# An LSTM step in which the input and cell gates take both halves of the state at once

## The reference

```python
# L0                                   # L1, per step
h = tanh(h @ Wh + x_t @ Wx + b)        h_bar = x_t @ Wx + b + h @ Wh
                                       i, f, o = sigmoid of h_bar[:, 0:256], [256:512], [512:768]
                                       g = tanh(h_bar[:, 768:1024])
                                       c = f * c + i * g;  h = o * tanh(c)
# L2: gates from means over the stream, two of four experts, and
shared = gelu(x @ sw1 + sb1) @ sw2 + sb2
# L3: adapters whose low-rank matrices come from cond
```

## Time and profile before

| | before |
|---|---|
| median of the runs (3, lowest to highest) | 1118.36 us (1118.17 to 1118.6) |
| profiled execution, its own time | 1117.36 us |
| its span, first to last instruction | 1115.4 us |
| mean granted clock of TensorE | 0.974 of full speed |
| busy: PE | 1079.2 us, 97% |
| busy: PEld | 979.4 us, 88% |
| busy: DVE | 818.1 us, 73% |
| busy: ACT | 586.4 us, 53% |
| busy: POOL | 279.3 us, 25% |

### The profile page before, as it was taken

The page is one execution under the profiler, slowest core; times in us unless marked ns, Lnnn a source line. Parts: engine busy times, 40 slices in busy tenths (PEclk is TensorE's granted clock), DMA queues, the critical chain, the costliest instruction groups (busy, mean ns, idle before and its releaser), DMA issues. The chain is left out here.

```text
span 1115.4 us, 54596 instructions
## 1 busy us (share of the span) xinstructions
PE 1079.2 (97%) x21946; PEld 979.4 (88%) x21946; DVE 818.1 (73%) x3458; ACT 586.4 (53%) x2147; POOL 279.3 (25%) x861
## 2 busy tenths in 40 slices
PE   6889999999999999999999998899999999999998
PEld 5889999999999999999999987688888888888877
DVE  7667877877877877777777676686666666676697
ACT  4456666566566566566565543433333333334486
POOL 3523323323333333333333320380000000000041
PEclk8759999999999999999999999999999999999999
DMA  8302120120220100000001110000000000000022
GB/s 258 103 23 59 56 63 25 56 65 23 61 60 26 57 18 29 14 23 23 9 4 27 16 15 12 1 2 2 2 2 2 2 1 2 2 3 2 4 90 82
DMA packets 54913, 36.91 MB, mean 33 GB/s; under 512 B 25560, under 2 KB 53514, under 8 KB 54668
## 3 DMA queue, kind: packets, MB, share of 16 engines
q1 hardware_dynamic: 54060, 33.12, 10.4%
q10 hardware_dynamic: 608, 0.30, 0.1%
HBM read 28.42 MB, written 4.98 MB: 30 GB/s over the span
## 5 line engine op out<-in xcount | busy, mean ns | idle before, releaser
L611 ACT ACTIVATE gel<-bank,seq 128x256 f32<-128x256 f32 x256 | 121.5, 475 | 214.7 <-PE bank L1253 211.9
L1251 PE MATMUL bank<-XHL,WE 128*128 128x256 f16 x768 | 209.9, 273 | 8.2 <-DVE XHL L842 3.4
L1251 PE MATMUL bank<-GH,WE 128*128 128x256 f16 x768 | 209.1, 272 | 2.4 <-DVE GH L868 2.0
L1253 PE MATMUL bank<-XHL,WE 128*128 128x256 f16 x768 | 209.8, 273 | 0.0
L1252 PE MATMUL bank<-XHL,WE 128*128 128x256 f16 x768 | 209.7, 273 | 0.0
L1253 PE MATMUL bank<-GH,WE 128*128 128x256 f16 x768 | 209.4, 273 | 0.0
L1252 PE MATMUL bank<-GH,WE 128*128 128x256 f16 x768 | 209.3, 273 | 0.0
L1363 PE MATMUL bank<-LH,seq 128*128 128x16 f16 x6144 | 194.4, 170 | 9.9 <-DVE LH L908 9.6
L1363 PEld LDWEIGHTS bank<-LH,seq 128*128 128x128 f16 x6144 | 171.5, 96 | 30.1 <-DVE LH L908 14.1
L428 POOL TENSOR_TENSOR RH<-rf,RH 128x32 f16<-128x32 f32 x256 | 63.7, 249 | 420.0 <-ACT RH L568 419.8
L1253 PE MATMUL bank<-seq 128*128 128x64 f16 (+2 forms) x1088 | 163.7, 208 | 0.0
(11 more groups left out here) (210 smaller groups left out, 2641.2 us busy)
## 6 DMA issues: line engine op xcount, KB each, us to landing
stage<-in_L_cond_ew SPq DMA_DIRECT2D x64, 128.0 KB, 2.1
stage<-in_L_cond_W SPq DMA_DIRECT2D x32, 256.0 KB, 3.6
XHL<-in_x SPq DMA_DIRECT2D x8, 512.0 KB, 9.0
out<-WE SPq DMA_DIRECT2D x16, 256.0 KB, 2.2
stage<-in_L_cond_sw SPq DMA_DIRECT2D x2, 1024.0 KB, 6.2
scratch<-rows SPq DMA_DIRECT2D x96, 8.0 KB, 2.1
stage<-in_L_cond_Wx SPq DMA_DIRECT2D x1, 1024.0 KB, 9.0
stage<-in_L_cond_Wh SPq DMA_DIRECT2D x1, 1024.0 KB, 11.1
```

The source lines that it names most:

```text
L611: nc.scalar.activation(gel[:, m % 2, :], banks[m % len(banks)][:, 0:256], ACT.Gelu_apprx_tanh, scale=scale, bias=bias).then_inc(s["a_g"], 1)
L1251: MM(out_, w(HI), x(HI), start=start, stop=False, skip_group_check=True)
L1253: return MM(out_, w(HI), x(LO), start=False, stop=stop, skip_group_check=True)
```

## The change

**The gates.** Each of the four tiles of input and cell gate takes 2 matmuls of 16 columns with the low half of the weights (line 1401 of the changed kernel) and 2 of 32 columns in which the state's high and low half stand side by side under the high half of the weights (1412). They leave two partial sums in PSUM. TensorE's order in a step is: input and cell gate with the low weights, the forget gate's high by high products (1407), the wait for `hl`, the 8 paired ones, `pe_ig`; the rest of the forget gate (1417, 1418), `pe_f`; the output gate as before (1425, 1429). That makes 36 matmuls a step in place of 44. VectorE's new `lstm_sum` (line 920, `zig`) adds the two sums, ScalarE takes one tangent of the forget gate (`tf`) and one of `zig` (`tig`).

**PSUM and x products.** Input and cell gate now fill two banks, the forget gate has one bank of four slots, the output gate one of two slots, each slot one turn of 4 steps. So the output gate's x products are made for 4 steps at a time, the seeds are three kinds, and TensorE has new waits: for the forget seed ahead of line 1407 (step 3 of each turn), for the output seed ahead of 1425 (step 1), for `oz` ahead of the output gate's x products, for a forget tangent ahead of the forget gate's.

**Order.** `lstm_sum` is the first instruction of a step on VectorE, `shared_lo` stands right behind it (it was behind the state update of the step before), and `HALVES` moves filling between steps.

```diff
-FIG_TILES = [2, 3, 0, 1, 6, 7]
+IG_TILES = [0, 1, 6, 7]
+F_TILES = [2, 3]
 O_TILES = [4, 5]
+NIG = len(IG_TILES)
+TURNS = T // H
+F_SLOTS, O_SLOTS = 4, 2
...
-        FIG, OB = bank[0:2], bank[2:4]
+        IG, FB, OB = bank[0:2], bank[2], bank[3]
         RB, HB, YB = bank[4], bank[5:7], bank[7]
...
                 n = blk * U + u
-                act.wait_ge(s["pe_fig"], n + 1)
-                nc.scalar.activation(tfig[:], FIG[u // H % 2][:, 0:6 * H * B].rearrange(
-                    "p (m t b) -> p m t b", m=6, t=H)[:, :, u % H, :],
-                    ACT.Tanh, scale=0.5 / S_LSTM).then_inc(s["a_fig"], 1)
+                act.wait_ge(s["pe_f"], n + 1)
+                slot = n // H % F_SLOTS
+                z = FB[:, slot * C * H * B:(slot + 1) * C * H * B].rearrange("p (m t b) -> p m t b", m=C, t=H)
+                nc.scalar.activation(tf[:].rearrange("p (m b) -> p m b", m=C), z[:, :, u % H], ACT.Tanh,
+                                     scale=0.5 / S_LSTM).then_inc(s["a_f"], 1)
+                act.wait_ge(s["v_zig"], n + 1)
+                nc.scalar.activation(tig[:], zig[:], ACT.Tanh, scale=0.5 / S_LSTM).then_inc(s["a_ig"], 1)
...
+            def seed(place_, tiles, done):
+                n = tiles.stop - tiles.start
+                act.wait_ge(s["p_gate_bias"], 6)
+                nc.scalar.activation(place_.rearrange("p (m t) -> p m t", t=H * B),
                                      gate_bias[:, tiles].rearrange("p (m o) -> p m o", o=1).to_broadcast(
-                                         [P, tiles.stop - tiles.start, steps * B]), ACT.Copy).then_inc(s[done], 1)
...
+            def seed_f(n):
+                turn = n // H
+                if n % H == 2 and 2 <= turn < TURNS - 2:
+                    act.wait_ge(s["a_tc"], n + 1)
+                    slot = (turn + 2) % F_SLOTS
+                    seed(FB[:, slot * C * H * B:(slot + 1) * C * H * B], bias_f, "a_f_seed")
+            def seed_o(n):
+                turn = n // H
+                if n % H == 0 and 1 <= turn < TURNS - 1:
...
+            def seed_ig(n):
+                turn = n // H
+                if n % H == H - 1 and turn < TURNS - 2:
...
                     if not last:
                         rnn_step(it + 1, u)
+                    seed_o(it * U + u)
                     if not first:
                         for m in done_tiles(u):
                             shared_full(it * M + m, m)
-                    seeds(it, u, last)
+                    seed_ig(it * U + u)
                     if it < NB - 2 and u in X_HI:
...
+            def lstm_sum(blk, u):
+                n = blk * U + u
+                dve.wait_ge(s["pe_ig"], n + 1)
+                V.reduce_sum(zig[:], IG[n // H % 2][:, :].rearrange("p (a m t b) -> p m t b a", a=2, m=NIG, t=H)[:, :, u % H],
+                             AX_X).then_inc(s["v_zig"], 1)
             def lstm_step(blk, u, rnn=True):
                 n = blk * U + u
                 slot = u % 2
                 hh = LH[:, slot, HI].rearrange("p c b -> p (c b)")
                 hl = LH[:, slot, LO].rearrange("p c b -> p (c b)")
-                tf, ti, tg = [tfig[:, 2 * k:2 * k + 2, :].rearrange("p c b -> p (c b)") for k in range(3)]
+                ti, tg = [tig[:, 2 * k:2 * k + 2, :].rearrange("p c b -> p (c b)") for k in range(2)]
                 x = X[:, :, :, bass.ds(blk * U + u, 1)].rearrange("p c b o -> p (c b o)")
-                dve.wait_ge(s["a_fig"], n + 1)
+                dve.wait_ge(s["a_f"], n + 1)
                 if n:
                     dve.wait_ge(s["v_c2"], n)
-                V.scalar_tensor_tensor(fc[:], tf, 1.0, c2[:], ALU.add, ALU.mult)
+                V.scalar_tensor_tensor(fc[:], tf[:], 1.0, c2[:], ALU.add, ALU.mult)
+                dve.wait_ge(s["a_ig"], n + 1)
                 V.scalar_tensor_tensor(ig[:], ti, 1.0, tg, ALU.add, ALU.mult).then_inc(s["v_ig"], 1)
                 dve.wait_ge(s["pe_o"], n + 1)
-                V.reduce_sum(oz[:], OB[u // G][:, :].rearrange("p (a m t b) -> p m t b a", a=2, m=C, t=G)[:, :, u % G],
-                             AX_X).then_inc(s["v_oz"], 1)
+                o_slot = n // H % O_SLOTS * 2 * C * H * B
+                V.reduce_sum(oz[:], OB[:, o_slot:o_slot + 2 * C * H * B].rearrange(
+                    "p (a m t b) -> p m t b a", a=2, m=C, t=H)[:, :, u % H], AX_X).then_inc(s["v_oz"], 1)
                 dve.wait_ge(s["v_ig"], n + 1)
...
@@ -1017,6 +1054,10 @@
             def block_steps(it, first, last, xr, matrix=False):
                 for u in range(U):
+                    lstm_sum(it, u)
+                    if not first:
+                        for m in done_tiles(u - 2) if u > 1 else ():
+                            shared_lo(it * M + m, m)
                     lstm_step(it, u, not last)
                     if last and u in extras:
                         extras[u]()
@@ -1024,8 +1065,6 @@
                         for k in range(4):
                             if u == (0 if last else SPLIT_WINDOWS[k]):
                                 split_x2(it - 1, k)
-                        for m in done_tiles(u - 1) if u else ():
-                            shared_lo(it * M + m, m)
                     for i in SHARED_PIECES[u] if first else ():
                         weight_lo(LSTM_SPLIT + i, shared_piece(i))
...
+                turn = n // H
                 old = (u + 1) % 2
-                def tile_at(bank_, steps, i, tile):
-                    at = i * steps * B + u % steps * B
-                    return bank_[:, at:at + B], tile
-                fig = [tile_at(FIG[u // H % 2], H, i, tile) for i, tile in enumerate(FIG_TILES)]
-                o = OB[u // G][:, :].rearrange("p (a m t b) -> p a m t b", a=2, m=C, t=G)[:, :, :, u % G]
-                if not isinstance(n, int) or n > 0:
+                w = lambda h, c, tile: LW[:, h, 1, c, tile * P:(tile + 1) * P]
+                z_ig = IG[turn % 2][:, :].rearrange("p (a m t b) -> p a m t b", a=2, m=NIG, t=H)[:, :, :, u % H]
+                at = turn % F_SLOTS * C * H * B
+                z_f = FB[:, at:at + C * H * B].rearrange("p (m t b) -> p m t b", m=C, t=H)[:, :, u % H]
+                at = turn % O_SLOTS * 2 * C * H * B
+                z_o = OB[:, at:at + 2 * C * H * B].rearrange("p (a m t b) -> p a m t b", a=2, m=C, t=H)[:, :, :, u % H]
+                if n > 0:
                     pe.wait_ge(s["v_hh"], n)
-                for z, tile in fig:
+                for i, tile in enumerate(IG_TILES):
                     for c in range(C):
-                        for h in (HI, LO):
-                            MM(z, LW[:, h, 1, c, tile * P:(tile + 1) * P], LH[:, old, HI, c],
-                               start=False, stop=False, skip_group_check=True)
-                if not isinstance(n, int) or n > 0:
+                        MM(z_ig[:, 0, i], w(LO, c, tile), LH[:, old, HI, c], start=False, stop=False,
+                           skip_group_check=True)
+                if u % H == 3 and 2 <= turn < TURNS - 2:
+                    pe.wait_ge(s["a_f_seed"], turn - 1)
+                for i, tile in enumerate(F_TILES):
+                    for c in range(C):
+                        MM(z_f[:, i], w(HI, c, tile), LH[:, old, HI, c], start=False, stop=False, skip_group_check=True)
+                if n > 0:
                     pe.wait_ge(s["v_hl"], n)
-                for z, tile in fig:
+                for i, tile in enumerate(IG_TILES):
                     for c in range(C):
-                        last = MM(z, LW[:, HI, 1, c, tile * P:(tile + 1) * P], LH[:, old, LO, c],
-                                  start=False, stop=(c == C - 1), skip_group_check=True)
-                last.then_inc(s["pe_fig"], 1)
+                        last = MM(z_ig[:, :, i], w(HI, c, tile), LH[:, old, :, c], start=False, stop=(c == C - 1),
+                                  skip_group_check=True)
+                last.then_inc(s["pe_ig"], 1)
+                for i, tile in enumerate(F_TILES):
+                    for c in range(C):
+                        MM(z_f[:, i], w(LO, c, tile), LH[:, old, HI, c], start=False, stop=False, skip_group_check=True)
+                        last = MM(z_f[:, i], w(HI, c, tile), LH[:, old, LO, c], start=False, stop=(c == C - 1),
+                                  skip_group_check=True)
+                last.then_inc(s["pe_f"], 1)
+                if u % H == 1 and 1 <= turn < TURNS - 1:
+                    pe.wait_ge(s["a_o_seed"], turn)
                 for i, tile in enumerate(O_TILES):
...
+            def ig_x(turn, i):
+                pe.wait_ge(s["p_x1l"], C * (turn + 1))
+                if turn >= 2:
+                    pe.wait_ge(s["a_ig_seed"], turn - 1)
+                lstm_x(IG[turn % 2][:, i * H * B:(i + 1) * H * B], IG_TILES[i], turn, turn < 2, i == 0)
+            def f_x(turn, i):
+                pe.wait_ge(s["p_x1l"], C * (turn + 1))
+                if turn >= F_SLOTS:
```

(31 more changed lines are left out.)

## The result

The changed kernel takes 1131.77 us (median of 4 runs, 1127.69 to 1132.66), the kernel before in the same comparison 1118.48 (1118.17 to 1119.08): ratio 1.0111, interval 1.0085 to 1.0137. It is slower by 13.3 us, where 6.8 were forecast. The profiled execution is the quickest of the four, 1127.69 with a span of 1125.8 against 1115.4.

A forecast was written before the change was run, and what follows sets the result against it. Bound: a four-engine loop, with TensorE's work almost equal. Terms 8 x 0.1 + 5 x 0.8 + 0 + 2 x 1 = +6.8 us on 1117.36 give 1124.2, median 1.0 above: 1125 us (+0.6%), range 1109 to 1136.

The forecast's parts named there:

- The loop through four engines: One LSTM step through TensorE, ScalarE and VectorE, 2.48 us without a free place, with TensorE's work a nearly equal limit.
- Steps 1 to 5: Loop of one step: paired matmuls at 0.64, sum at 1.02 taking 0.28, product at 1.62, step 2.36 instead of 2.47.
- The rival of a quicker sum: From last paired matmul to second tangent: sum quicker than priced, so the change gains, 1106 to 1113 us; chance 0.17.
- The sixteen steps: Steps 0 to 15 of a block with weights: -0.31 and +1.10 against before, +0.8 us a block.
- 8 x 0.1 + 5 x 0.8: Blocks with low-rank work at +0.1 us each, and blocks 9 to 13 at +0.8 each.
- I give each +1 (ends -2 and +3): Blocks 0 and 15, whose other tails were not worked out step by step: +1 us each.
- the rival: TensorE idles longer, granted clock falls: 10 us for one block, 150 for all, 1135 to 1270 us; chance 0.05.
- my signs of being wrong: Sums under 0.25, a `shared_lo` not pushing the product, steps all 2.36, or granted clock under 1.00 between 110 and 650 us.
- That gives back 0.7: Steps 13 and 14 of low-rank blocks, with less filling in 12 and 13: 2.75 and 2.70, from about 3.0 and 3.14.

The follow-up runs named there:

- two tables: Variant without pairing or sum (44 matmuls), with the new filling table in blocks 0 to 8 and the old one in 9 to 15: 1109.97 us, ratio 0.9926.
- first profile: Profiled execution of the changed kernel in its first comparison with the kernel before: 1127.69 us, span 1125.8 against 1115.4.
- second profile: Changed kernel unaltered, run and profiled a second time: median 1131.55 us, ratio 1.0119; its profiled execution has a span of 1130.2.

## Why the prediction came out as it did

**Which limit, right.** The loop through four engines and TensorE's work lie on each other. Shorten the loop alone (44 matmuls, no sum): no change with the new table, 8.7 us with two tables, and TensorE is full in both. Fewer matmuls, with the sum in the loop: slower, with TensorE at 94%. Both (36 matmuls, no sum): 1083.8. No run has fewer matmuls and the old loop, so TensorE's part alone is not shown. One reading was off: the scan, from the first hh to the last, is 655 of 1115 us, 59% and not two thirds.

**The loop, right.** Steps 1 to 5 gave 0.64, 1.02, a sum of 0.28, 1.62 and 2.36; measured 0.57, 0.98, 0.27 to 0.29, 1.59 and 2.33. The low half is ready a little earlier when its write takes 0.19, as in the step shown, and not 0.25, as in 131 of the 256 steps; the quiet steps of block 14 are accordingly about 2.33 or 2.39, on both sides of the forecast. The rival of a quicker sum falls with this.

**The sixteen steps, right in the sum, mixed one by one.** Change against before (first profile, mean of blocks 9 to 13, from consecutive starts of lines 908 and 945):

| step | forecast | measured | | step | forecast | measured |
|---|---|---|---|---|---|---|
| 0 | +0.08 | +0.16 | | 9 | +0.05 | -0.05 |
| 1 | +0.31 | +0.31 | | 10 | +0.11 | -0.04 |
| 2 | -0.12 | -0.02 | | 11 | +0.08 | +0.11 |
| 3 | +0.10 | +0.10 | | 13 | +0.14 | +0.10 |
| 4, 8, 12 | -0.14 | -0.13 | | 14 | -0.05 | -0.06 |
| 5, 7 | +0.16 | +0.12 | | 15 | +0.01 | -0.05 |
| 6 | +0.06 | +0.10 | | sum | +0.8 | +0.65 |

Low-rank blocks were forecast at +0.1 and measured at +0.17, block 14 at 0 and -0.3. So the terms of these 14 blocks, 8 x 0.1 + 5 x 0.8, came to 4.8, and measured 4.3. That the sums agree so well is in part luck: step 0 came out 0.08 longer than forecast and step 10 0.15 shorter, and in the low-rank blocks steps 13 and 14 gave back 0.83 and not 0.7, while step 15 lost 0.21 where 0.01 was forecast.

**Blocks 0 and 15, mis-sized.** The step of the prediction that failed in size is "I give each +1 (ends -2 and +3)", for tails that I had not worked out: +3.0 (at the upper end) and +2.1. Both follow the same rule as the rest. In block 0 the weight halves wait for ScalarE and then hold the sum; moved, block 0 is at 40.7. In block 15 the add of the shared network waits for TensorE's filling, and the sum stands behind it; moved, its step 15 is at 2.36. About 1.0 of the 1.1 by which this step grew (3.56 to 4.66) is the new table, which puts a second filling half there: with the old one the add waits until 1.72 and not 2.71, and the step is at 3.67 (changed kernel with the old table, VectorE, hh at 697.17):

```profile
698.89 0.69 DVE L890 SCALAR_TENSOR_TENSOR X<-bank,X 128x512 f32<-128x512 f32 x1 [1.07 <-PE bank L1292]
...
700.84 0.19 DVE L945 SCALAR_TENSOR_TENSOR LH<-to,tc 128x32 f16<-128x32 f32 x1 [0.32 <-ACT tc L595]
```

The two blocks together are 5.1 where 2 was given: 3.1 of the 3.5 us by which the span grew more than the 6.8 forecast. The other 3 us up to 13.3 lie between the profiled executions and the medians: the first profile of the changed kernel is 4.1 below its median, that of the kernel before 1.1 below.

**The clock, not as the rival had it.** I had priced a block at the lower level at 10 us and gave it 0.05. What comes are falls of a few microseconds, most at the end of a block and not in every execution, 0.7 to 1.0 us each where they lengthened a step. They were no term of my sum, and a granted clock under 1.00 between 110 and 650 us, which the second profile has, stood among my signs of being wrong. In that profile they make 3.6 of the 4.4 us over the first; that they also make the 4 us between the first profile and the median of its comparison is likely and not shown: those executions have no profile, and the mean clock of an execution does not tell (0.965 at 1127.69 and at 1131.07). The Trainium skill (TensorE: Matmul & The Clock Gate, section "What's actually happening") calls the throttled state the default, which only activity releases; the traces agree only in part, with a fall behind 2.18 of 3 us busy in one execution and none behind 2.08 of 3 in another.

**The table, wrong in its worth.** "That gives back 0.7" was right for steps 13 and 14 (forecast 2.75 and 2.70, measured 2.61 and 2.67), but the old table in the same kernel has 41.36 a low-rank block against 41.60: what is relieved in two steps is lost in ScalarE's three and elsewhere.

## What to carry to other kernels

In a loop through several engines, an added short instruction costs its own length and hand-overs in every step, and more by where it stands: it turns one free stretch of its engine into two, and side work that fitted into the one overruns both. Here, of the 48 us between the changed kernel and the one without the sum, 13 came back by moving such work and changing the table; 35 did not. Before such a change, list what the engine does in that stretch and put each piece on the side where it ends in time; then work out the first and the last round as well. When two limits lie on each other, test each alone, on the chip: of the variants that leave no product out, only the loop shortened at unchanged matmuls, with the old filling in the late blocks, was faster than both kernels (1110.0 against 1118.7).

## What the runs showed of the hardware

A fall of the clock can come behind short holes: after TensorE had been busy 2.18 of 3 us, with no gap above 0.5, the granted clock went to its lower level for a few microseconds (0.72, 0.50, 0.50 and 0.58 in the four from 455 on), and the step behind it took 3.39 in place of 2.42. The same program did not show it in another execution, with the same holes. The kernel before, with TensorE busy 526.7 of the 530 us from 110 to 640, kept 1.00 in all of them.
